# Decoder layer, attention stage: key differences left in PSUM, reciprocals of 8 columns through DRAM, the last tile of each half summed by TensorE

## What is computed

```
q, k, v = (proj(Wq), proj(Wk), proj(Wv))
scores = jnp.einsum('bhqd,bhkd->bhqk', q, k)
bias = rel_bias[_relative_position_buckets(S)]
scores = scores + bias.transpose(2, 0, 1)[None]
attn = jax.nn.softmax(scores, axis=-1)
ctx = jnp.einsum('bhqk,bhkd->bhqd', attn, v)
ctx = ctx.transpose(0, 2, 1, 3).reshape(B, S, H * DK)
return ctx @ Wo.T
```

## Time and profile before

| what | value |
|---|---|
| time, median of 3 runs | 4750.68 us (4736.71 to 4769.41) |
| the profiled execution: its own time | 4765.34 us |
| its span in the profile | 4763.6 us |
| TensorE | 4146.0 us busy (87%) |
| VectorE | 2993.0 us (63%) |
| GpSimd | 2632.9 us (55%) |
| ScalarE | 2056.1 us (43%) |
| attention heads 0 to 31 in the span | about 350 to 3430 us |

### The profile page before, as it was taken

The page is one execution under the profiler, slowest core; times in us unless marked ns, Lnnn a source line. Parts: engine busy times, 40 slices in busy tenths (PEclk is TensorE's granted clock), DMA queues, the critical chain, the costliest instruction groups (busy, mean ns, idle before and its releaser), DMA issues. The chain is left out here.

```text
span 4763.6 us, 59079 instructions
## 1 busy us (share of the span) xinstructions
PE 4146.0 (87%) x18740; PEld 2219.1 (47%) x18740; DVE 2993.0 (63%) x3677; ACT 2056.1 (43%) x3407; POOL 2632.9 (55%) x1279
## 2 busy tenths in 40 slices
PE   8868999999989999999899998999769898984499
PEld 6734444444444444444444444444356666662244
DVE  3246777777777777777777777777346666663400
...
DMA packets 236461, 282.30 MB, mean 59 GB/s; under 512 B 92523, under 2 KB 134507, under 8 KB 235368
## 3 DMA queue, kind: packets, MB, share of 16 engines
...
## 5 line engine op out<-in xcount | busy, mean ns | idle before, releaser
L230 POOL TENSOR_TENSOR acc<-acc,probs 128x1024 f32<-128x1024 f32 x896 | 2160.1, 2411 | 539.5 <-ACT probs L623 373.7
L626 ACT ACTIVATE probs<-ps,far_bias 128x1024 f32<-128x1024 f32 (+7 forms) x1280 | 1022.7, 820 | 1401.5 <-DVE near_s L739 799.6
L713 DVE TENSOR_REDUCE maxes<-ps 128x1 f32<-128x1024 f32 x1024 | 1246.1, 1217 | 474.8 <-PE ps L438 468.3
L438 PE MATMUL ps<-stacks 64*128 64x512 f32 x2048 | 770.6, 457 | 291.5 <-DVE maxes L713 285.6
L473 PE MATMUL ps<-probs,v_head 128*64 128x512 f32 x4096 | 1001.4, 610 | 1.9 <-ACT probs L623 1.9
L453 PE MATMUL ps<-stacks 64*128 64x512 f32 x1792 | 701.9, 456 | 0.0
L452 PE MATMUL ps<-stacks 128*128 128x512 f32 x2048 | 627.5, 423 | 0.1
L453 PEld LDWEIGHTS ps<-stacks 64*128 64x128 f32 x1792 | 280.7, 185 | 530.3 <-issue 308.8
L438 PEld LDWEIGHTS ps<-stacks 64*128 64x128 f32 x2048 | 312.0, 191 | 445.9 <-DVE maxes L713 401.5
L473 PEld LDWEIGHTS ps<-probs,v_head 128*64 128x64 f32 x4096 | 250.0, 137 | 489.1 <-issue 486.3
L452 PEld LDWEIGHTS ps<-stacks 128*128 128x128 f32 x2048 | 356.8, 191 | 218.7 <-issue 164.6
...
## 6 DMA issues: line engine op xcount, KB each, us to landing
stacks<-c_k SPq DMA_DIRECT2D x128, 256.0 KB, 2.4
stacks<-c_q SPq DMA_DIRECT2D x128, 256.0 KB, 2.5
stacks<-c_d SPq DMA_DIRECT2D x256, 128.0 KB, 2.3
...
stacks<-c_q SPq DMA_DIRECT2D x128, 128.0 KB, 2.3
...
scr_ctx<-ctx_out SPq DMA_DIRECT2D x128, 128.0 KB, 2.3
...
```

The costliest lines, as they stand in the source:

```text
L230: pool.tensor_tensor(acc[:, qb, :], acc[:, qb, :], pr, ALU.add).then_inc(s["summed"], 1)
L438: mm = pe.matmul(ps[:, MX + i, :], stacks[0:64, mside, QA, qt * P:(qt + 1) * P], stacks[0:64, mside, KX, kc * 512:(kc + 1) * 512], start=T ...
L626: ins = act.activation(probs[:, st % PT_RING, a:z], sc[:, a:z], ACT.Exp, bias=bias)
L713: dve.tensor_reduce(maxes[:, qt, pair:pair + 1], ps[:, MX:MX + 2, :], AX.XY, ALU.max).then_inc(s["max_done"], 1)
```

## The change

- `step` leaves the key difference in `PB` itself (`ps[0:64]`), over the queries, once these are out; `step_hi` and `step_lo` read it there. `dk` is gone. `step` and `step_lo` stand together in the group after the evacuation, and the next projection waits for `step_lo` (the bank is held longer).
- ScalarE copies the queries between its exponentials and the keys (two copies) behind the second. VectorE's `queries_low` stands at the end of the group, behind the second `near` and the second `largest`.
- `sum_of` moves to groups 8 and 0. GpSimd adds 15 of 16 tiles, and TensorE takes the last one straight from `probs`: 4 matmuls of 512 columns with 2 weight loads each instead of 2.
- The sums go by transfers: one row of each half is spread over 128 partitions as 128 x 8 (`part`), VectorE takes a reciprocal of 128 x 8 (groups 9 and 1), the result goes to DRAM (`scr_inv`) and comes back copied over 64 partitions (`sums`); `context` follows in groups 10 and 2.
- The negated maxima go to DRAM and back, element by element, in place of TensorE's turn and VectorE's copy.
- On SP the new function `divisors` stands behind `fill` and the loads of a head.

```diff
-TURN_GROUPS = {12: 0, 4: 1}
-SUM_GROUPS = {12: 0, 4: 1}
-RECIP_GROUPS = {13: (0, 0), 14: (0, 2), 5: (1, 0), 6: (1, 2)}
-PIECES = 4
-PIECE_COLS = 512 // PIECES
+SUM_GROUPS = {8: 0, 0: 1}
+RECIP_GROUPS = {9: 0, 1: 1}
+CONTEXT_GROUPS = {10: 0, 2: 1}
+PART = 2 * 512 // P
...
-                    if kt == 0:
+                    if kt in (0, NT - 1):
...
             def guard(m, side, half):
                 sp.wait_ge(s["neg_ready"], 2 * m + half + 1)
+                sp.sem_inc(s["held"], 1)
+                past(sp, s["neg_in"], 16 * (2 * m + half))
+                sp.dma_start(scr["neg"][half].rearrange("(p t) -> p t", p=P), neg_max[:, half * 8:half * 8 + 8].bitcast(F32)).then_inc(s["neg_stored"], 16)
+                sp.wait_ge(s["neg_stored"], 32 * m + 16 * half + 16)
                 sp.dma_start(stacks[0:1, side, QB, half * QW:(half + 1) * QW].bitcast(F32).rearrange("o (t p) -> o t p", p=P),
-                             neg_row[:, half, :].bitcast(F32)).then_inc(s["neg_in"], 16)
+                             scr["neg"][half].rearrange("(o p t) -> o t p", o=1, p=P), allow_slow_non_contiguous=True).then_inc(s["neg_in"], 16)
...
+            def divisors(n, qb):
+
+                sp.wait_ge(s["sum_out"], 2 * n + qb + 1)
+                for half in range(2):
+                    rows = slice(64 * half, 64 * half + 64)
+                    sp.dma_start(part[rows, :], sums[64 * half:64 * half + 1, :].rearrange("o (p c) -> o p c", c=PART)).then_inc(s["spread"], 16)
+                sp.wait_ge(s["recip"], 2 * n + qb + 1)
+                sp.sem_inc(s["held"], 1)
+                past(sp, s["recip_in"], 64 * n + 32 * qb)
+                sp.dma_start(scr["inv"][qb].rearrange("(p c) -> p c", c=PART), part_inv[:]).then_inc(s["recip_stored"], 16)
+                sp.wait_ge(s["recip_stored"], 32 * n + 16 * qb + 16)
+                for half in range(2):
+                    sp.dma_start(sums[64 * half:64 * half + 64, :],
+                                 scr["inv"][qb, half * 512:(half + 1) * 512].partition_broadcast(64)).then_inc(s["recip_in"], 16)
...
                     sp.dma_start(w_in[:], io["wqk"][h_weights]).then_inc(s["w_in"], 16)
-                    xn_block(0, reload)
+                if carry:
+                    divisors(n - 1, 1)
                 if own:
                     guard(n, side, 1)
-                if h_weights is not None:
-                    xn_block(1, reload)
                 if carry:
                     store_ctx(n - 1, 1)
                 if h_weights is not None:
-                    xn_block(2, reload)
+                    xn_block(0, reload)
+                    xn_block(1, reload)
+                if own:
+                    divisors(n, 0)
                 if nxt:
                     guard(n + 1, 1 - side, 0)
                 if own:
                     store_ctx(n, 0)
+                if h_weights is not None:
+                    xn_block(2, reload)
                 if h_weights is not None:
                     xn_block(3, reload)
...
-                    past(pe, s["k_hi"], 4 * m + tb)
-                    past(pe, s["step"], 4 * m + tb)
-                    if tb == 1:
+                    past(pe, s["step_lo"], 4 * m + tb)
+                    if tb == 0:
                         past(pe, s["sum_out"], 2 * (m - 2))
-                    if tb == 3:
+                    if tb == 2:
                         past(pe, s["sum_out"], 2 * (m - 2) + 1)
-                    if tb == 1:
-                        past(pe, s["neg_ready"], 2 * (m - 2) + 2)
-                    if tb == 3:
-                        past(pe, s["neg_ready"], 2 * (m - 1) + 1)
...
-            def sum_of(n, qb):
+            def sum_of(n, qb, stepped):
+                pe.wait_ge(s["step_lo"], stepped)
+                past(pe, s["sum_out"], 2 * n + qb)
                 pe.wait_ge(s["summed"], n * STEPS + NT * (qb + 1))
-                pe.matmul(ps[0:64, PB, :], ones[:], acc[:, qb, 0:512], start=True, stop=True)
-                pe.matmul(ps[64:128, PB, :], ones[:], acc[:, qb, 512:1024], start=True, stop=True).then_inc(s["summ"], 1)
+                last = probs[:, (NT - 1) % PT_RING, :]
+                for half in range(2):
+                    cols = slice(half * 512, (half + 1) * 512)
+                    pe.matmul(ps[64 * half:64 * half + 64, PB, :], ones[:], acc[:, qb, cols], start=True, stop=False)
+                for half in range(2):
+                    cols = slice(half * 512, (half + 1) * 512)
+                    mm = pe.matmul(ps[64 * half:64 * half + 64, PB, :], ones[:], last[:, cols], start=False, stop=True)
+                mm.then_inc(s["summ"], 1)
...
-                    if g in TURN_GROUPS:
-                        half = TURN_GROUPS[g]
-                        if own if half else nxt:
-                            m = n if half else n + 1
-                            pe.wait_ge(s["turn_in"], 2 * m + half + 1)
-                            if prep:
-                                pe.wait_ge(s["k_hi"], 4 * (n + 2) + g // 4)
-                                pe.wait_ge(s["step"], 4 * (n + 2) + g // 4)
-                            pe.transpose(ps[0:NT // 2, PB, 0:P], neg_max[:, half * 8:half * 8 + 8], ident[:]).then_inc(s["turn_done"], 1)
...
+                    if g == 0 and prep:
+                        split_w(n + 2)
                     if own:
                         exp(n, k, side, 2 * g)
-                    if g == 0 and prep:
-                        split_w(n + 2)
                     if prep and g in EVAC_GROUPS:
-                        take_out(n + 2, EVAC_GROUPS[g])
+                        queries_out(n + 2, EVAC_GROUPS[g])
...
+                    if prep and g in EVAC_GROUPS:
+                        keys_out(n + 2, EVAC_GROUPS[g])
...
+            def step(m, tb):
+
                 dve.wait_ge(s["k_hi"], 4 * m + tb + 1)
-                past(dve, s["step_lo"], 4 * m + tb)
-                dve.tensor_tensor(dk[:], ps[64:128, PB, :], c_d[64:128, tb * 512:(tb + 1) * 512], ALU.subtract).then_inc(s["step"], 1)
+                dve.wait_ge(s["q_lo"], 4 * m + tb + 1)
+                dve.tensor_tensor(ps[0:64, PB, :], ps[64:128, PB, :], c_d[64:128, tb * 512:(tb + 1) * 512], ALU.subtract).then_inc(s["step"], 1)
 
             def step_lo(m, tb):
 
                 cols = slice(tb * 512, (tb + 1) * 512)
                 dve.wait_ge(s["step_hi"], 4 * m + tb + 1)
-                dve.tensor_tensor(c_k[64:128, cols].bitcast(F32R), dk[:], c_d[0:64, LOOKBACK + tb * 512:LOOKBACK + (tb + 1) * 512],
+                dve.tensor_tensor(c_k[64:128, cols].bitcast(F32R), ps[0:64, PB, :], c_d[0:64, LOOKBACK + tb * 512:LOOKBACK + (tb + 1) * 512],
                                   ALU.subtract).then_inc(s["step_lo"], 1)
 
-            def reciprocals(n, qb, first):
-                if first == 0:
-                    dve.wait_ge(s["sum_out"], 2 * n + qb + 1)
-                for piece in (first, first + 1):
-                    cols = slice(piece * PIECE_COLS, (piece + 1) * PIECE_COLS)
-                    dve.reciprocal(sums[:, cols], sums[:, cols]).then_inc(s["recip"], 1)
+            def reciprocals(n, qb):
+
+                dve.wait_ge(s["spread"], 64 * n + 32 * qb + 32)
+                past(dve, s["recip_stored"], 32 * n + 16 * qb)
+                dve.reciprocal(part_inv[:], part[:]).then_inc(s["recip"], 1)
 
             def context(n, qb):
 
-                dve.wait_ge(s["recip"], (n * QBLK + qb + 1) * PIECES)
+                dve.wait_ge(s["recip_in"], 64 * n + 32 * qb + 32)
                 dve.wait_ge(s["ctx_raw"], 2 * n + qb + 1)
                 dve.tensor_tensor(ctx_out[:], ctx_out[:], sums[:], ALU.mult).then_inc(s["ctx"], 1)
 
             def head(n, k, side):
                 carry, own, nxt, prep = parts(n)
                 for g in range(GROUPS):
+                    stepped = None
+                    if g in SPLIT_GROUPS:
+                        tb = SPLIT_GROUPS[g]
+                        if tb < BLOCKS - 1 and prep:
+                            stepped = (n + 2, tb)
+                        if tb == BLOCKS - 1 and nxt:
+                            stepped = (n + 1, tb)
                     if has_max(n, g):
                         largest(n, side, g, 0)
                     if own:
                         near(n, k, side, 2 * g)
-                    if g in TURN_GROUPS:
-                        half = TURN_GROUPS[g]
-                        if own if half else nxt:
-                            rows(n if half else n + 1, half)
-                    if prep and g in EVAC_GROUPS:
-                        low_parts(n + 2, EVAC_GROUPS[g])
+                    if stepped:
+                        step(*stepped)
                     if own:
                         near(n, k, side, 2 * g + 1)
                     if has_max(n, g):
                         largest(n, side, g, 1)
+                    if stepped:
+                        step_lo(*stepped)
```

(19 more changed lines are left out.)

42 lines of the change are left out of this document (22 added, 20 removed).

## The result

| what | before | after |
|---|---|---|
| median | 4743.69 us (4735.03 to 4769.41, 4 runs) | 4792.85 us (4790.15 to 4794.45, 4 runs) |
| the profiled execution: its own time | 4765.34 us | 4792.67 us |
| its span | 4763.6 us | 4790.9 us |
| TensorE busy | 4146.0 us (87%) | 4195.6 us (88%) |
| VectorE busy | 2993.0 us (63%) | 2602.7 us (54%) |

The ratio after to before is 1.0094, 95% interval 1.0052 to 1.0136. VectorE lost 390 us of work, GpSimd 170 us, and the kernel became 49 us longer by the medians. It also became steadier: its executions lie within 4.3 us, those of before within 34.

A forecast was written before the change was run, and what follows sets the result against it. The prediction took TensorE as the bound: 95.5 - 11.0 - 0.6 + 1.9 + 2.5 = 88.3 us a head, plus 10.0 for the waits and clock, 98.3. With 29 heads at +1.9 and +9 elsewhere: 4750.7 + 64 = 4814 us, range 4765 to 4865.

The forecast's parts named there:

- The long wait: End of group 1: VectorE's reciprocal stands 8.1 us for `part`, queued late on SP; TensorE's pair loses 6.8 us.
- The second wait: End of group 2: `context` waits for its loads from DRAM, costing TensorE 2.3 us more a head.
- The clock: After TensorE's 6.8 us stall its clock falls to half; 0.9 us a head, a quarter of 3.6.
- VectorE's chain hides most of the slower work: Behind the stall, VectorE's work up to 30.0 us covers most half-clock matmuls, leaving 0.9 of 3.6 us.
- the second rival: Half clock after every stall costs 3.6 us instead of 0.9, `context` 1 more: 4922 us; chance 0.21.
- The removed stalls: TensorE's waits before group 0 and in groups 3, 7, 9, 11, 15 all go: 11.0 us a head.
- the other small waits: New TensorE waits from the changed order: 0.5 us in group 0, 0.3 in 4, 0.2 in 8, 0.8 in 12.
- The added matmuls: Two more `sum_of` matmuls a half on TensorE cost 0.93 us each time, 1.86 a head, not hidden.
- The turns: TensorE's two turns of the maxima a head go away, saving an estimated 0.3 us each.
- only the first wait costs: Rival: `context` finds GpSimd pausing and the clock stays up; 95.1 us a head, 4722 us; chance 0.22.
- the clock costs in full: Rival: half clock after every stall, 3.6 us, plus 1 for `context`; 102.0 a head, 4922 us; chance 0.21.
- Long wait hidden: Rival: SP is through within 5 us after block 3; 88.3 us a head, 4525 us; chance 0.05.

The follow-up runs named there:

- e1: The kernel after, with the second half's reciprocal in group 4 instead of 1 and its `context` in group 6 instead of 2: 4519.65 us.
- e3: The kernel after, with the `part` transfers issued inside `fill`, ahead of block 3's lookback copies, and `context` in group 4; reciprocal still in group 1: 4535.45 us.
- e2: The kernel after, with only the second half's `context` moved, to group 4 instead of 2: 4806.01 us.
- e7: The kernel of e1 with GpSimd adding all 16 tiles and two sum matmuls a half: 4475.38 us.
- e6: The kernel of e1 with `queries_low` again ahead of the second bias addition and ScalarE's three copies together between its exponentials: 4613.42 us.
- e5: The kernel of e1 with the key difference in SBUF again (`dk`), the bank held just as long: 4621.34 us.
- e11: The kernel of e1 with full-size reciprocals on VectorE in groups 13, 14, 5 and 6, and no transfers of the divisors: 4528.83 us.

## Why the prediction came out as it did

**The long wait: right, step by step.** Counted from the end of `step_lo`, the prediction has `w_in` issued after 11.8 us, the reciprocal starting at 15.3 and the pair of TensorE at 16.7; the trace has 11.8, 15.5 and 16.9. VectorE stands for 8.3 us (8.1 predicted), the pair is 6.9 late (6.8). The place, the transfer named and the work queued behind are as forecast, and e1 and e3 show that they are the cause.

**The second wait: wrong.** I had put 2.3 us on `context`. In group 2 of the rows above it starts at 2324.46 and waits for nothing, 0.6 us before TensorE is at the next pair. The store of `scr_inv` lands 1.4 us after its issue, not 2.3, the loads 2.9, not 3.4. `context` starts 0.2 us ahead of GpSimd's next addition (2324.66), so it takes 0.68 (median of all 64: 679 ns) instead of the 1.39 taken. Even as late as forecast it would have cost little: the prediction has the reduction behind it through 30.0 us after the start of group 0 (2297.92 here), and the pair that needs it is at 30.6 (2328.48), kept back by the slow clock. e2 shows that moving it gains nothing.

**The clock: the step "VectorE's chain hides most of the slower work" failed.** In the head shown, the half clock costs 1.75 us in one batch of values (3.61 instead of 1.86) and 0.48 in each of two pairs (1.15 from 2320.29 to 2321.44, instead of 0.67): 2.7. On the median of the heads group 2 is 9.35 us longer than a plain one, 6.9 of them the stall, which leaves 2.4. I had taken 0.9, a quarter of the 3.6 of the earlier trace rows; it was two thirds, since with `context` not waiting nothing hid it. The two errors, 2.3 too much and 1.5 too little, come from one mistake (which of two things ends last there) and partly cancel: the head was to be 98.3 us and is 98.0. That it comes out so close is in part luck. The rule cited for the second rival, from the Trainium skill's "TensorE: Matmul & The Clock Gate", section "HAM oscillation — how this bites in real kernels", holds here: the low clock came back in every head. The rival that rested on it took 3.6 us for it, half as much again as the 2.4.

**The removed stalls: right.** Groups 3, 7, 9 and 15 came down, and plain groups stay at 5.25. Without the long wait a head takes 88.9 us in e1, against 88.3 predicted. The difference is mainly group 11, where 1.35 us remain of which I had allowed 0.7; group 7 keeps 0.2, and the other small waits (0.6 in group 0, 0.3 in group 4, 0.4 in group 8, 0.5 in group 12) add up to the 1.8 allowed. The reason in group 11 is not the four transfers ahead of `context`, which I had named. It is that `neg_max` or `context` stays beside GpSimd's addition until this ends (2371.44 in the rows below; timeline of VectorE, then TensorE, in the kernel after):

```profile
2369.00 2.46 DVE L747 TENSOR_SCALAR neg_max<-max_q,far_bias 128x8 fp32r<-128x8 f32 x1
2371.38 0.68 DVE L788 TENSOR_TENSOR ctx_out<-ctx_out,sums 128x512 f32<-128x512 f32 x1
2371.99 1.21 DVE L736 TENSOR_REDUCE maxes<-ps 128x1 f32<-128x1024 f32 x1
...
2373.25 0.50 PE L457 MATMUL ps<-stacks 64*128 64x512 f32 x1 [0.86 <-DVE maxes L736]
```

In 28 of heads 1 to 29 one of the two takes 2.35 us or more in group 10, and group 11 takes 6.6; in head 29 both are short (0.23 and 0.69), and it takes 5.26, a plain group.

A slip of naming changes no sum: TensorE's pair at 2306.09 in the earlier trace rows, called the second of group 3, is the first pair of group 4, which waits for VectorE's work of group 3; in the same way show group 6 and the start of group 7.

**The added matmuls: right.** 0.87 each time in e7 against 0.93. **The turns** were not tried alone. Group 4 of before takes 5.43, 4.32 of it for a plain group without its four projection matmuls (0.93) and 0.87 for the sums, which leaves about 0.25 for a turn, against 0.3 taken.

**The sum.** Between the two profiled executions (4790.9 - 4763.6 = 27.3 us; predicted 64):

| part | predicted | measured |
|---|---|---|
| up to the first scores of head 0 | +11 | -3.1 |
| head 0 | -8 | -12.4 |
| heads 1 to 29 | +55 | +36.3 |
| head 30 | +6 | +2.9 |
| head 31 and all behind it | 0 | +3.6 |

The forecast is 37 us above the trace here. 14 of them are the eight projection blocks ahead of head 0, whose two new waits did not show at all; what covers them stays open. 10 are a wrong base: I divided by 30 a stretch that ends with head 30, which is 10 us shorter than the others. Heads 1 to 29 of before take 96.74 us and not 96.4, so 98.3 would have been +1.6 each. 9 are the 0.3 us between 98.3 and 98.0 in 29 heads. Head 0 gained 4 more, since its 99.9 us before were above an average head's. The rest nearly cancels: head 30 was 3 us less than forecast, and what is behind head 31 was 4 more.

The step from the profiled execution to the median hid part of this. The profiled execution of before was 14.7 above its median, and I took these 14.7 off the result. But they fit falls of the clock in some heads (10 of heads 1 to 29 of the profiled execution took 98 us or more, the others about 95.5; of 21 later executions of before, the one at 4741.67 us had a granted clock of 0.957 and the one at 4775.67 of 0.949). A kernel whose clock falls in every head has no such play: its profiled execution is on its median. So medians differ by 49 where the profiles differ by 27. 37 us too much in the sum and 14.7 too little in this step nearly make up the 21 us between the forecast of 4814 and the 4793 measured: it came out closer than its parts, by luck. The result lies in the forecast's own range and 5 us below its line for "slower" (4798): the chances had favoured slower (0.54) over within 1% (0.34). The direction was right, at 0.94% with an interval of 0.52 to 1.36%.

**The rivals.** Of "only the first wait costs" the half about `context` was right and the half about the clock wrong; of "the clock costs in full" the reverse. "Long wait hidden" is what e1 and e3 make of it: 4525 predicted, 4520 and 4535 measured. `step_lo` takes 685 ns, so the short form came.

**Where the 7.9 us a head between before and e1 come from,** as far as the runs separate them, each taken back alone from e1: the order (e6) 2.9 and the form of `step_lo` in PSUM (e5) 3.2 gained, the added matmuls (e7) 1.7 lost, the short reciprocals (e11) 0.4 gained, which the times can't tell from nothing. The remaining 3 hold the keys' difference moved one group on, the turns, the new groups of the sums, and the clock's falls of before (96.74 against 95.53, so about 1.2). They were not tried one by one, and it is not shown that the parts simply add up.
